# Delta rule on one core: the second half's values issued behind the first half's sums on TensorE, and every fourth token's queries read from PSUM by VectorE

## What is computed

```python
Ui = inv @ (Vi - Bi @ W_t)
W_new = W_t + KiT @ Ui
...
O_i = Qi @ W_avg * a + Qi @ W_t * c + T_mat * (Qi @ KiT) @ Ui
```

## Time and profile before

| what | us |
|---|---|
| median of 3 runs | 1977.03 |
| lowest and highest | 1974.11, 1977.23 |
| profiled execution, its own time | 1973.72 |
| its span in the trace | 1971.9 |
| DVE busy in the span | 1473.6 (75%) |
| PE busy | 1611.2 (82%) |
| ACT busy | 1185.5 (60%) |
| POOL busy | 1093.7 (55%) |

### The profile page before, as it was taken

The page is one execution under the profiler, slowest core; times in us unless marked ns, Lnnn a source line. Parts: engine busy times, 40 slices in busy tenths (PEclk is TensorE's granted clock), DMA queues, the critical chain, the costliest instruction groups (busy, mean ns, idle before and its releaser), DMA issues. The chain is left out here.

```text
span 1971.9 us, 50860 instructions
## 1 busy us (share of the span) xinstructions
PE 1611.2 (82%) x17727; PEld 1253.2 (64%) x17727; DVE 1473.6 (75%) x4099; ACT 1185.5 (60%) x2763; POOL 1093.7 (55%) x1141
## 2 busy tenths in 40 slices
PE   5599999999689697699847777777789607999995
PEld 5478888887577543344415555555578607999994
DVE  7688888888489743699979999999778624555556
ACT  4566666666279821587737888888466504555552
POOL 3378888887000178233247888888637773444440
PEclk8799999999899789799969999999876658999997
DMA  3000000000511123521000000000321112222217
GB/s 120 19 3 4 3 4 4 3 4 3 209 41 41 33 47 43 149 67 43 12 0 1 1 1 1 1 1 1 128 82 50 52 59 66 66 63 66 66 52 262
DMA packets 84954, 92.34 MB, mean 47 GB/s; under 512 B 11696, under 2 KB 69296, under 8 KB 84000
## 3 DMA queue, kind: packets, MB, share of 16 engines
q1 hardware_dynamic: 67840, 62.66, 10.0%
q0 software_dynamic: 14560, 22.24, 4.2%
q10 hardware_dynamic: 2304, 4.20, 0.6%
HBM read 46.14 MB, written 42.91 MB: 45 GB/s over the span
## 5 line engine op out<-in xcount | busy, mean ns | idle before, releaser
L2284 POOL TENSOR_TENSOR delta_A<-delta_A,delta_sW 128x256 f32<-128x256 f32 x256 | 193.6, 756 | 78.6 <-ACT delta_sW L2131 52.1
L2054 PE MATMUL delta_u<-delta_m,tables_sb 128*128 128x256 f32 x512 | 166.1, 406 | 82.0 <-DVE delta_m L2204 82.0
L697 ACT ACTIVATE attn_p_att<-attn_score,attn_mx 128x32 f32<-128x32 f32 (+7 forms) x512 | 150.2, 409 | 133.7 <-DVE attn_mx L759 133.6
L2911 POOL DMA_INDIRECT choice_rows<-ffn_y,ffn_xg x135 | 129.4, 959 | 167.9 <-DVE ffn_y L3018 164.4
L2131 ACT ACTIVATE delta_sW<-delta_W,tables_sb 128x256 f32<-128x256 f32 x256 | 126.6, 506 | 79.1 <-DVE delta_W L2226 75.2
L2054 PEld LDWEIGHTS delta_u<-delta_m,tables_sb 128*128 128x128 f32 x512 | 87.0, 189 | 132.3 <-DVE delta_m L2204 125.6
L2050 PE MATMUL delta_u<-delta_v_own,tables_sb 128*128 128x256 f32 x512 | 153.6, 382 | 9.6 <-DVE xnT L2191 9.6
L2868 POOL DMA_INDIRECT rows<-mix_rows,mix_slot x128 | 125.4, 979 | 47.0 <-issue 39.4
L1327 POOL DMA_INDIRECT exp_rows<-rows,slot_token x32 | 32.6, 1020 | 190.0 <-issue 190.0
L2226 DVE TENSOR_TENSOR delta_W<-delta_W,delta_u 128x128 f32<-128x128 f32 x512 | 133.6, 282 | 4.5
L2213 DVE TENSOR_TENSOR delta_u<-delta_u,delta_prod 128x256 f32<-128x256 f32 x256 | 109.9, 429 | 17.2 <-PE delta_u L2054 3.3
(11 more groups left out here) (397 smaller groups left out, 4693.0 us busy)
## 6 DMA issues: line engine op xcount, KB each, us to landing
ffn_xg<-rows SPq DMA_DIRECT2D x135, 66.0 KB, 1.8
acc<-route_zero SPq DMA_DIRECT2D x10, 832.0 KB, 15.5
comb_rows<-choice_rows SPq DMA_DIRECT2D x32, 256.0 KB, 5.2
rows<-route_rows SPq DMA_DIRECT2D x8, 640.0 KB, 3.6
load_rows<-in_x SPq DMA_DIRECT2D x16, 256.0 KB, 3.7
bT<-acc SPq DMA_DIRECT2D x16, 256.0 KB, 3.9
qT<-acc SPq DMA_DIRECT2D x16, 256.0 KB, 4.5
x_kept<-xT SPq DMA_DIRECT2D x16, 256.0 KB, 2.1
```

The source lines that it names most:

```text
L697: last = nc.scalar.activation(p_att[:, gr, PAIR_OFF[n]:PAIR_OFF[n] + SLOT * (n + 1)], S[:, gr, c:c + SLOT * (n + 1)], ACT.Exp, bias=mx[:, ...
L2054: nc.tensor.matmul(corrections(h, pp % 2), g.t("same_head"), m1[:, h].rearrange("p t d b -> p (t d b)"), start=False, stop=True).then_inc( ...
L2284: nc.gpsimd.tensor_tensor(A[:, t % 8], A[:, (t - 1) % 8], sW[:, t % RING], ALU.add).then_inc(k.A, 1)
L2911: nc.gpsimd.indirect_dma_start(g.choice_rows, bass.IndirectOffsetOnAxis(xg[:, n % RING, D:D + 1].bitcast(U32), 0), y[:, n % RING, :], None ...
```

## The change

Two things change.

1. On PE, values(1) of pair p is issued behind correct(0) of the same pair p, and no longer behind correct(1) of pair p-1. So correct(0) of the next pair stands directly behind correct(1).
2. The queries of each quad's fourth token are no longer copied to `q_rows` in SBUF. A new ACT instruction, queries_of_last, writes them to 64 free columns of the `b_ps` bank that the group does not use for its own rates, and last_of_quad reads them there. The copy to `q_rows` (rows_of_queries) covers three tokens of four, and no longer waits for last_of_quad; the new instruction waits for that instead, and for the products of the group before.

```diff
+        def by_quad(x, group):
+            quads = x[:, :].rearrange("p (b n t) -> p n t b", n=QUADS, t=QUAD)
+            return quads[:, 2 * group:2 * group + 2]
+
+        def last_queries(group):
+            return b_ps[(group + 1) % 2][:, GT * B:GT * B + 2 * B].rearrange("p (n b) -> p n b", b=B)
...
-            for h in range(2):
-                values(0, 0, h)
+            values(0, 0, 0)
...
                     correct(i, pp, 0)
+                    values(i, pp, 1)
                     if not final:
                         values(*following, 0)
                     if pair >= LATER and (pair - LATER) % 2 == 1:
                         outputs((pair - LATER) // 2, (pair - LATER) // 2 % 2)
                     correct(i, pp, 1)
-                    if not final:
-                        values(*following, 1)
...
             def rows_of_queries(group):
                 if group > 1:
                     act.wait_ge(k.m3, 2 * (group - 1))
+                nc.scalar.activation(q_rows[:, group % 2].rearrange("p (n t) b -> p n t b", t=QUAD)[:, :, 0:QUAD - 1],
+                                     by_quad(g.qT, group)[:, :, 0:QUAD - 1], ACT.Copy).then_inc(k.q_rows, 1)
+
+            def queries_of_last(group):
+                for h in range(2):
+                    if group > 0:
+                        act.wait_ge(by_half[h].m1, 4 * group)
+                if group > 1:
                     act.wait_ge(k.m3_last, 2 * (group - 1))
-                nc.scalar.activation(q_rows[:, group % 2], by_token(g.qT, GT * group, GT), ACT.Copy).then_inc(k.q_rows, 1)
+                nc.scalar.activation(last_queries(group), by_quad(g.qT, group)[:, :, QUAD - 1], ACT.Copy).then_inc(k.q_last, 1)
...
+                    if place == 0:
+                        queries_of_last(group)
                     if place == 0 and group + 1 < T // GT:
                         rates((group + 1) // 2, (group + 1) % 2)
...
                 if quad % 2 == 0:
-                    dve.wait_ge(k.q_rows, quad // 2 + 1)
+                    dve.wait_ge(k.q_last, quad // 2 + 1)
                 at = quad % 2 * QUAD + QUAD - 1
-                query = q_rows[:, quad // 2 % 2, at][:, None, :].to_broadcast([128, DH1, B])
+                query = last_queries(quad // 2)[:, quad % 2][:, None, :].to_broadcast([128, DH1, B])
```

More of the change, by code:

```diff
@@ L1996, in delta_phase @@
         out_ps = [s.ps(f"out{n}") for n in range(2)]
-        k = s.sems("zeroed product overlap cut less pairs_ready b_in v_rows v_in k_rows q_rows scaled A m3 m3_last out_made evac")
+        k = s.sems("zeroed product overlap cut less pairs_ready b_in v_rows v_in k_rows q_rows q_last scaled A m3 m3_last out_made evac")
         by_half = [s.sems("m1 u m2 W", h) for h in range(2)]
```

## The result

The changed kernel takes 1945.24 us (median of 4 runs, 1943.27 to 1946.01), against 1975.57 us for the kernel before on the same chips (4 runs). The ratio is 0.9847, 95% interval 0.9831 to 0.9862: 1.5% faster, 30 us. The profiled execution took 1945.79 us, 27.9 less than that of before.

What follows compares the result with a forecast made beforehand. DVE was taken as the bound, slowed by last_of_quad meeting POOL and by PE's queue. Savings of 30.7, 0.8 and 0.3 us make 31.8: 1973.72 becomes 1941.9, plus 3.3 for the median, 1945; range 1939 to 1958.

Steps and rivals of the forecast that it cites:

- the sum: Over the pair loop: four pairs take 10.66 us against 11.65; with the first pairs and the end, 31.8 us gained.
- DVE bounds, PE's queue hides in it: Steady loop: DVE, 93% busy, sets the pace, but PE's queue sets pair length; moving values cuts odd pairs to 2.61 us.
- The queries' price: last_of_quad reading its query from PSUM: 418 ns each, bounds 418 and the present mean of 702.
- PE late on even pairs: Outputs ahead of correct(1) leave PE free 0.04 us late; nothing taken for it, bounds nothing and 2.5 us.
- The rival "slower": PE reaches correct(1) late behind values(1): up to 0.43 us a pair, 55 us, ending at 2018; chance 0.03.
- ACT: 32 new query instructions, about 0.27 us each, and shorter copies: 5 us more work, hidden in ACT's idle time.
- POOL: Additions and product take 5.26 us a quad, under the 5.33 of two new pairs; 99% full, the next bound.
- the rival "only one half works": Only one edit pays: short last_of_quad alone gains 14 us (1963), the values' move alone 15 us (1962); chance 0.10.
- the share of 14 us that the sum takes from last_of_quad: Even pairs: the 31 lasting 3.25 us fall to 2.80 once last_of_quad is short, 14 us.

## Why the prediction was right, and the step in it that was not

The time was right (1945 forecast, 1945.24 measured), and the sum over the changed kernel nearly so. The account of which edit brings what was wrong. That the median was hit so closely is partly luck. I had forecast 31.8 us of gain; the profiled execution gained 27.9 and the medians 30.3. A group of four pairs came out 0.06 us over my 10.66, 1.9 us over 31 groups, and from the end of the last last_of_quad to the end of the span are 563.8 us where they were 561.3. In the medians a part of this is made up by the kernel before, whose median on four runs is 1.5 us under the 1977.03 that I had subtracted from.

- **DVE bounds, PE's queue hides in it: right.** The odd pairs fell from 2.80 to 2.60 and 2.66, 2.61 forecast. The 0.05 over it in every second one is product(0): in the odd pair above it starts 1.44 us after change(0), where the earlier trace rows have 1.39. It is the first product of a new group, which also waits for that group's rates. Before, PE's queue covered that.
- **The queries' price: right.** 411 to 422 ns against 418 taken. By my estimate from the page of the Trainium skill that I had set against it, "VectorE: DVE Perf Modes", the section on the TRN2 errata, the PSUM form would have been 65 ns above the SBUF form. The trace doesn't bear it out for this shape: in PSUM it took 411 to 422 ns, and in SBUF, where POOL held nothing back, 416 to 426.
- **PE late on even pairs: mis-sized, and without effect.** I had PE free 0.04 us late; correct(1) starts 0.18 us after its product ended, 0.13 more than the 0.05 of a PE that stands ready. I had 0.1 us to spare, and that was just used up: change(1) on even pairs is at 2.05 (1189.76 to 1191.81), where last_of_quad and PE both let it go. The two runs with values(1) twice show the room in each: about 0.43 us or more in odd pairs, none in even ones. The rival "slower" was nearer than its chance said: one more values matmul in even pairs took back 26.4 of the 29.4 us.
- **ACT: right.** The new instruction took 316 ns (0.27 estimated) and the copy 525; its idle time for states fell from 68.4 us in 360 to 36.3 in 330. POOL waited 9.9 us for it, and DVE not at all.
- **POOL: right.** Its product is at 1.80 to 1.83 us, and it is the next bound.
- **The failed step is the rival "only one half works"**, and with it the share of 14 us that the sum takes from last_of_quad. The long form in the earlier trace rows was real, and its price was right while the values stood where they were (13.4 us). But I took its frequency, every second one, as a property of that instruction, and priced the move alone at 15 us. It was a property of how POOL and DVE stood to each other. The move alone took 29.4 us.

What decides is the order in which the two meet. The Trainium skill says on its page "SBUF — State Buffer", in the section on who interferes with whom, that a VectorE instruction with two SBUF inputs contends with a GpSimd instruction that reads SBUF, and that the one that issues first blocks the other. The traces agree in both directions: 0.87 to 0.95 us for last_of_quad behind an addition, 1.72 us in place of 1.59 for two additions behind it. They also give the size. In the four kernels with the query in SBUF and last_of_quad on DVE, every held last_of_quad (73 of them) ended 0.28 us behind the end of POOL's instruction, wherever it had started. So one that starts in the last 0.14 us of an addition loses nothing of its 0.42, one that starts 0.06 us into it takes 0.95, and the last one, behind the product of 1.80 us, 2.01. The other way round a held addition ended 0.58 to 0.59 us behind the end of last_of_quad, which cost POOL up to 0.28 us. Before, the two orders took turns. With the move alone DVE is so fast that POOL hardly waits for ACT (1.3 us of 330), and its additions settle where last_of_quad starts at the end of one. For POOL's being full as what holds this place there is one run only: with less work on POOL the long ones came back, 0.87 us every second time, and the stretch grew by 14.8 us. That run also shortened the product that stands between the additions, so the load isn't the only thing that changed. Why the place is just there I can't show; a second cause for it isn't excluded.

So, once the values are moved, the PSUM queries bring nothing to the stretch. They take away a dependence on luck: with them the stretch stays at 340 to 341 whether POOL is full or not, and the last last_of_quad no longer stands 2.0 us behind POOL's last product.

## What to carry to other kernels

Two engines that share a path can meet in an order that costs one of them several times what the other order costs its partner, and a change elsewhere can flip that order; before two such edits are given a price each, run each alone, and run them with the other engine's load changed. A wait can hide in the overlap of pipelined rows, without any row that names it: the start of the next instruction against the end of what feeds it shows it. Before a piece of work is split to spread it, look whether its parts already run side by side: a cut across them saves nothing.

## What the runs showed of the hardware

Four matmuls of 32 columns each that write different 32-partition slots ran side by side: in the trace of the changed kernel their passes start in fours, 0.007 us apart, and the fours 0.11 us apart. 16 passes of 128 columns took 0.64 us, 8 passes on two of the slots 0.63, and 8 passes on all four 0.43. Unhindered, a 128x256 f32 product on VectorE took 418 ns with both operands in SBUF and 412 to 418 with one in PSUM (medians). A last_of_quad with both operands in SBUF that began in the last 0.06 us of GpSimd's addition wasn't held; one that began 0.06 to 0.14 us behind its start was held for 0.45 to 0.53, and ended 0.28 us behind it.
